# Rotary part of layer 1: ScalarE exchanges the halves, VectorE takes the cosine product, GpSimd the sine product

## The chip, the cores and the metric

One core of a Trainium2 chip runs the whole kernel. The metric is the device time of one execution in microseconds. Before the change it was 678.48 (median of 3 runs, 677.88 to 679.29).

## The reference

The kernel computes four transformer layers on x of 1024 tokens by 256, each layer an attention and a feed-forward part on the same layer norm, added to x. The change is in layer 1's attention: 16 heads of 128 dimensions, rotary embedding on queries and keys, a causal window of 128.

```python
def _apply_rotary(x, cos, sin):
    d2 = x.shape[-1] // 2
    x1, x2 = (x[..., :d2], x[..., d2:])
    return jnp.concatenate([x1 * cos - x2 * sin, x2 * cos + x1 * sin], axis=-1)
...
q = split_heads(hidden_states @ wq)
k = split_heads(hidden_states @ wk)
v = split_heads(hidden_states @ wv)
...
q = _apply_rotary(q, cos, sin)
k = _apply_rotary(k, cos, sin)
valid = (k_pos > q_pos - WINDOW) & (k_pos <= q_pos)
attn = jnp.einsum('bhqd,bhkd->bhqk', q, k) * scale
attn = jnp.where(valid, attn, neg)
attn = jax.nn.softmax(attn, axis=-1)
out = jnp.einsum('bhqk,bhkd->bhqd', attn, v)
return out.transpose(0, 2, 1, 3).reshape(Bsz, Ln, NUM_HEADS * HEAD_DIM) @ wo
```

## The kernel before

The program is written by hand, one queue for each engine; the order in the code is the order of execution, and semaphores tie the queues together. There is no scheduler.

Layer 1 goes head by head (H1 = 16; the first 14, SPLIT, run in loops over pairs, then come the routed and shared experts, then heads 14 and 15). While head h is finished, the queries and keys of head h+1 are prepared. These are four pieces j = 0 to 3, each of 128 dimensions (partitions) by 512 tokens: keys and queries of tokens 0 to 511, then of tokens 512 to 1023. A piece takes this way:

- TensorE projects it (project_qk) into bank j % 2, six products with split weights (L625 to L627). For j = 2 and 3 it first waits until the piece that was in the bank has been read (rope_half).
- ScalarE copies the bank to SBUF (keep_raw, L1349) and counts raw_kept.
- VectorE multiplies the bank by the sine, with the two halves of the partitions exchanged: two instructions of 64 partitions (rotate, L1775 and L1776). The second counts rope_half, which frees the bank.
- GpSimd multiplies ScalarE's copy by the cosine (turn_qk, L2270), waits for rope_half and adds the two (L2275) into kT1 or qT1. That counts qk_ready, for which the scores wait (L821).

Beside this, for head h: row maxima of the scores on VectorE (row_max, L1785), exponents on ScalarE (L1368) in four groups g, transposes of the probabilities on TensorE (turn_probs, L835), their copies on ScalarE (keep_pT, L1335 to L1338), products with the values (L850, L851), the outputs' leading part on ScalarE (keep_oT, L1342) and its rest on VectorE (rest_of_oT, L1792), the output projection on TensorE (project_out, L625 to L627 with 256 columns) and its sum into x on VectorE (L1801).

The weights are split too. ScalarE rounds them (round_wqk L1355, round_wv, round_wo), GpSimd computes the rest (L2232, named rest_of_wqk, rest_of_wv, rest_of_wo) and counts wqk_split, wv_split, wo_split, for which TensorE waits; in heads 11 to 13 VectorE does it for the query and key weights (L1937). Heads come in pairs: behind the second of a pair TensorE also projects the values of the next pair (project_v), and ScalarE copies them (L1330).

VectorE also does the routing of the experts beside the heads: top-k rounds (L1756, L1761) in heads 0 to 8, the last of them and the weights of tokens (L1808 to L1819) in head 9, the row numbers (L1825 to L1839) behind head 10. GpSimd sends rows with indirect DMAs (L2298) in heads 11 to 13 and fetches them (L2303) in heads 14 and 15.

## Time and profile before

| | |
|---|---|
| median of 3 runs | 678.48 us |
| profiled execution, own time | 678.17 us |
| its span, first to last instruction | 676.4 us |
| TensorE busy | 643.2 us, 95% |
| weight loads busy | 504.0 us, 75% |
| VectorE busy | 534.5 us, 79% |
| ScalarE busy | 344.5 us, 51% |
| GpSimd busy | 336.2 us, 50% |
| mean granted TensorE clock | 0.997 |

The busy times are of one profiled execution. PE is TensorE, PEld its weight loads, DVE VectorE, ACT ScalarE, POOL GpSimd; L12 is line 12 of the kernel before. Matmuls are pipelined and their ends are modelled, so that a row of TensorE is best read by its start and the start of the next. Names such as arena, zone and bank are the program's storage: a bank is one of the eight PSUM banks, the others are SBUF.

### The profile page before, as it was taken

To read this page: it belongs to the slowest core of one execution; us is meant where nothing else is said; L and a number is where in the kernel's file an instruction comes from. 1 tells how busy PE (TensorE), PEld (TensorE's weight loads), DVE (VectorE), ACT (ScalarE), POOL (GpSimd) and SP (SyncE) were. 2 spreads that over 40 slices of the span, in tenths; PEclk is the share of its full clock that TensorE was granted. 3 is DMA by queue.
4 is the path that set the end of the run, shared out by engine and by line. 5 is a ranking of instruction groups with operands and counts; after the bars stand their busy time and mean duration, and the time that the engine had idled before them with its cause. 6 is when DMAs were issued, how large, how long until landed. Compare 5 with 4: busy or idle time off the path is not lost.

```text
span 676.4 us, 13522 instructions
## 1 busy us (share of the span) xinstructions
PE 643.2 (95%) x4852; PEld 504.0 (75%) x4852; DVE 534.5 (79%) x1080; ACT 344.5 (51%) x750; POOL 336.2 (50%) x267
## 2 busy tenths in 40 slices
PE   8998999999899999999999999999999999879987
PEld 4446888788478988888898787987868747647766
DVE  4378777698599998988989997667457899679993
ACT  1596212300556485655647564485445583379441
POOL 1063555591457667474866736978429633310000
PEclk9999999999999999999999998999999999999999
DMA  8801000000601001010100101101421300100001
GB/s 258 347 0 64 2 1 1 2 0 0 241 17 41 24 8 39 16 39 23 39 23 8 39 16 50 48 24 30 157 70 48 71 1 0 40 0 1 1 0 63
DMA packets 14792, 31.38 MB, mean 46 GB/s; under 512 B 1853, under 2 KB 8603, under 8 KB 14173
## 3 DMA queue, kind: packets, MB, share of 16 engines
q1 hardware_dynamic: 13069, 27.25, 12.2%
q0 software_dynamic: 1536, 3.15, 1.8%
q8 instruction: 28, 0.46, 0.3%
q10 hardware_dynamic: 144, 0.40, 0.2%
q14 instruction: 15, 0.12, 0.1%
HBM read 26.59 MB, written 5.24 MB: 47 GB/s over the span
## 4 chain that ended last, share of the span: by engine, by line
PE 58%; DVE 16%; issue 11%; ACT 10%; DMA 3%; POOL 2%; SPq 0%; DVEq 0%; POOLq 0%; ACTq 0%
PE bank L625 10%; PE bank L626 8%; PE bank L627 8%; PE bank L615 7%; PE bank L606 5%; PE bank L821 3%; PE bank L851 3%; PE bank L850 2%; PE bank L835 2%; DVE arena L1776 2%; DVE x L1801 2%; DVE arena L1775 2%; PE bank L648 1%; DMA arena<-in_w1s 1%; PE bank L724 1%
## 5 line engine op out<-in xcount | busy, mean ns | idle before, releaser
L625 PE MATMUL bank<-zone 128*128 128x256 f32 (+1 forms) x472 | 167.4, 355 | 12.8 <-DVE arena L1776 3.6
L626 PE MATMUL bank<-zone 128*128 128x256 f32 (+1 forms) x472 | 156.5, 331 | 0.0
L627 PE MATMUL bank<-zone 128*128 128x256 f32 (+1 forms) x472 | 156.3, 331 | 0.0
L625 PEld LDWEIGHTS bank<-zone 128*128 128x128 f32 x472 | 88.8, 188 | 37.8 <-issue 14.6
L2270 POOL TENSOR_TENSOR arena<-arena 128x512 f32<-128x512 f32 x64 | 82.6, 1291 | 63.2 <-ACT arena L1349 63.2
L627 PEld LDWEIGHTS bank<-zone 128*128 128x128 f32 x472 | 89.1, 189 | 9.1
L2275 POOL TENSOR_TENSOR arena<-arena 128x512 f32<-128x512 f32 x64 | 83.8, 1310 | 23.5 <-DVE arena L1776 13.0
L626 PEld LDWEIGHTS bank<-zone 128*128 128x128 f32 x472 | 89.2, 189 | 5.3
L1368 ACT ACTIVATE arena<-arena 128x256 f32<-128x256 f32 (+1 forms) x128 | 62.1, 487 | 30.0 <-DVE arena L1785 29.4
L1785 DVE CUSTOM_DVE_ANT_0 arena<-bank,const 128x256 f32<-128x256 f32 (+1 forms) x128 | 45.7, 404 | 20.0 <-PE bank L821 19.0
L1801 DVE SCALAR_TENSOR_TENSOR x<-bank,arena,x 128x256 f32<-128x256 f32 x128 | 53.0, 473 | 7.4 <-PE bank L627 6.8
L1775 DVE TENSOR_TENSOR arena<-bank,arena 64x512 f32<-64x512 f32 x64 | 44.3, 693 | 16.6 <-ACT arena L1349 15.1
L1349 ACT ACTIVATE arena<-bank 128x512 f32<-128x512 f32 x64 | 37.5, 586 | 28.0 <-PE bank L627 27.9
L851 PE MATMUL bank<-arena 128*128 128x128 f32 x256 | 49.5, 275 | 0.0
L2232 POOL TENSOR_TENSOR zone<-arena,zone 128x512 fp32r<-128x512 f32 (+1 forms) x39 | 40.5, 1047 | 10.8 <-ACT zone L1433 5.1
L850 PE MATMUL bank<-arena 128*128 128x128 f32 x224 | 44.9, 282 | 0.0
L1776 DVE TENSOR_TENSOR arena<-bank,arena 64x512 f32<-64x512 f32 x64 | 43.7, 684 | 0.8
L1330 ACT ACTIVATE arena<-bank 128x512 f32<-128x512 f32 x32 | 19.1, 598 | 48.3 <-PE bank L627 48.3
L851 PEld LDWEIGHTS bank<-arena 128*128 128x128 f32 x256 | 39.9, 191 | 1.9 <-ACT arena L1336 0.6
L821 PE MATMUL bank<-arena 128*32 128x160 f32 x896 | 40.9, 307 | 0.0
L2378 POOL TENSOR_TENSOR arena<-arena,minus_half 128x4 f32<-128x4 f32 x2 | 2.0, 1012 | 75.3 <-DVE arena L2080 75.3
L1088 PE MATMUL bank<-zone 128*128 128x512 f32 x128 | 34.4, 407 | 4.3 <-DVE plain L2062 2.2
(300 smaller groups left out, 1342.1 us busy)
## 6 DMA issues: line engine op xcount, KB each, us to landing
arena<-in_qk SPq DMA_DIRECT2D x16, 256.0 KB
arena<-in_tern SPq DMA_DIRECT2D x1, 3072.0 KB, 21.4
arena<-in_wv SPq DMA_DIRECT2D x8, 256.0 KB, 2.9
arena<-in_wo SPq DMA_DIRECT2D x16, 128.0 KB, 2.1
arena<-in_wr SPq DMA_DIRECT2D x1, 1792.0 KB, 9.9
lB<-in_lB SPq DMA_DIRECT2D x1, 1288.5 KB, 24.0
xg_rows<-arena SPq DMA_DIRECT2D x1, 1024.0 KB
arena<-in_cossin SPq DMA_DIRECT2D x2, 512.0 KB, 5.2
```

What stands on the lines that cost most here:

```text
L625: pe.matmul(dst, lhi, rhi, start=(n == 0), stop=False)
L626: pe.matmul(dst, lhi, rlo, start=False, stop=False)
L627: last = pe.matmul(dst, llo, rhi, start=False, stop=(n == len(terms) - 1 and not open_end))
L821: last = pe.matmul(ps[2 + g % 2][rows_out, at:at + P + 32], qT1[:, t * P + 32 * i:t * P + 32 * i + 32], kT1[:, t * P - P + 32 * i:t * P + ...
L850: pe.matmul(ps[6 + g // 2][:, tok(t % TPB)], v1[:, t - 1, mine], pT1[:, t, 0, :], start=True, stop=False)
L851: last = pe.matmul(ps[6 + g // 2][:, tok(t % TPB)], v1[:, t, mine], pT1[:, t, 1, :], start=(t == 0), stop=True)
L1368: last = act.activation(S1[:, t, lo:], S1[:, t, lo:], ACT.Exp, scale=-1.0, bias=nmax[:, t:t + 1], accum_out=rsum[:, t:t + 1])
L1775: dve.tensor_tensor(qsin[0:64, j, :], ps[j % 2][64:128, :], sinT[64:128, at], ALU.mult)
L1776: dve.tensor_tensor(qsin[64:128, j, :], ps[j % 2][0:64, :], sinT[0:64, at], ALU.mult).then_inc(rope_half, 1)
L1801: last = dve.scalar_tensor_tensor(out=x[:, t, :], in0=ps[bank][:, tt * D:(tt + 1) * D], scalar=rinv[:, t:t + 1], in1=x[:, t, :], op0=ALU.m ...
L2270: pool.tensor_tensor(qraw[:, j, :], qraw[:, j, :], cosT[:, at], ALU.mult).then_inc(cos_done, 1)
L2275: pool.tensor_tensor((kT1, qT1)[j % 2][:, at], qraw[:, j, :], qsin[:, j, :], ALU.add).then_inc(qk_ready, 1)
```

## The change

ScalarE now copies a piece with its halves exchanged, as two copies of 64 partitions. VectorE multiplies the bank by the cosine in one instruction on 128 partitions, and GpSimd multiplies the exchanged copy by a sine table whose signs are exchanged as well. Three orders change with it. On ScalarE the first turned probabilities come ahead of the raw copy of piece 1, and at the end of a head the order is: turned probabilities 2 and 3, first output copy, rounded query and key weights, raw copy of piece 3, second output copy. On VectorE rotation 3 stands behind the first rest of the output. On GpSimd the rest of the query and key weights stands between pieces 2 and 3.

```diff
@@ tables and buffers
-        qsin = m.grid(4, BW)
+        qcos = m.grid(4, BW)
...
-        qraw = m.grid(4, BW)
+        qturn = m.grid(4, BW)
...
-    cossin = np.concatenate([np.tile(np.cos(freq), (2, 1)), np.concatenate([np.sin(freq), -np.sin(freq)], 0)], 1).astype(f32)
+    cossin = np.concatenate([np.tile(np.cos(freq), (2, 1)), np.concatenate([-np.sin(freq), np.sin(freq)], 0)], 1).astype(f32)
@@ ScalarE, keep_raw
-                act.activation(qraw[:, j, :], ps[j % 2], ACT.Copy).then_inc(raw_kept, 1)
+                act.activation(qturn[0:64, j, :], ps[j % 2][64:128, :], ACT.Copy)
+                act.activation(qturn[64:128, j, :], ps[j % 2][0:64, :], ACT.Copy).then_inc(raw_kept, 1)
@@ ScalarE, head
                     if g == 2:
+                        keep_pT(h, 0, base)
                         if more:
                             keep_raw(h + 1, 1)
-                        keep_pT(h, 0, base)
                         keep_pT(h, 1, base)
...
                 if more:
                     keep_raw(h + 1, 2)
                 keep_pT(h, 2, base)
+                keep_pT(h, 3, base)
+                keep_oT(h, 0, base)
+                if more_v:
+                    round_wqk(h + 2)
                 if more:
                     keep_raw(h + 1, 3)
-                keep_oT(h, 0, base)
-                keep_pT(h, 3, base)
                 keep_oT(h, 1, base)
                 if more_v:
-                    round_wqk(h + 2)
                     if c:
                         keep_v(pair + 1)
@@ VectorE, rotate
-                dve.tensor_tensor(qsin[0:64, j, :], ps[j % 2][64:128, :], sinT[64:128, at], ALU.mult)
-                dve.tensor_tensor(qsin[64:128, j, :], ps[j % 2][0:64, :], sinT[0:64, at], ALU.mult).then_inc(rope_half, 1)
+                dve.tensor_tensor(qcos[:, j, :], ps[j % 2], cosT[:, at], ALU.mult).then_inc(rope_half, 1)
@@ VectorE, head
                 if more:
                     rotate(h + 1, 2)
-                    rotate(h + 1, 3)
...
                 for b in range(NB):
                     rest_of_oT(h, b)
+                    if more and b == 0:
+                        rotate(h + 1, 3)
@@ GpSimd, turn_qk
-                    pool.tensor_tensor(qraw[:, j, :], qraw[:, j, :], cosT[:, at], ALU.mult).then_inc(cos_done, 1)
-                    pool.wait_ge(cos_done, h * 4 + (j + 1))
+                    pool.tensor_tensor(qturn[:, j, :], qturn[:, j, :], sinT[:, at], ALU.mult).then_inc(sin_done, 1)
+                    pool.wait_ge(sin_done, h * 4 + (j + 1))
...
-                    pool.tensor_tensor((kT1, qT1)[j % 2][:, at], qraw[:, j, :], qsin[:, j, :], ALU.add).then_inc(qk_ready, 1)
+                    pool.tensor_tensor((kT1, qT1)[j % 2][:, at], qturn[:, j, :], qcos[:, j, :], ALU.add).then_inc(qk_ready, 1)
@@ GpSimd, beside_head
-                turn_qk(h + 1, (2, 3), base)
+                turn_qk(h + 1, (2,), base)
+                if weights:
+                    rest_of_wqk(h + 2)
+                turn_qk(h + 1, (3,), base)
```

ScalarE's queue in the loop, first head of a pair, from the copy of piece 2 to the end of the head. The line numbers are of each kernel's own file. Before:

```order
L1349 ACTIVATE arena<-bank 128x512
L1333 REGISTER_ALU
L1338 ACTIVATE arena<-bank 128x512
L1346 REGISTER_ALU
L1349 ACTIVATE arena<-bank 128x512
L1341 ISA
L1342 ACTIVATE zone<-bank 128x512
L1338 ACTIVATE arena<-bank 128x512
L1342 ACTIVATE zone<-bank 128x512
L1352 ISA
L1354 REGISTER_ALU
L1355 ACTIVATE zone<-arena 128x512
```

The same place in the changed kernel, from the second copy of piece 2:

```order
L1350 ACTIVATE arena<-bank 64x512
L1333 REGISTER_ALU
L1338 ACTIVATE arena<-bank 128x512 x2
L1341 ISA
L1342 ACTIVATE zone<-bank 128x512
L1353 ISA
L1355 REGISTER_ALU
L1356 ACTIVATE zone<-arena 128x512
L1346 REGISTER_ALU
L1349 ACTIVATE arena<-bank 64x512
L1350 ACTIVATE arena<-bank 64x512
L1342 ACTIVATE zone<-bank 128x512
```

The copy of piece 3 has moved behind both turned probabilities, the first output copy and the rounded weights (L1356), and stands right ahead of the second output copy (L1342).

VectorE's queue in the same head, from the last top-k operation to the output's second rest. Before:

```order
L1761 MATCH_REPLACE arena<-arena 7x1024
L1772 REGISTER_ALU
L1774 REGISTER_ALU
L1775 TENSOR_TENSOR arena<-bank,arena 64x512
L1776 TENSOR_TENSOR arena<-bank,arena 64x512
L1772 REGISTER_ALU
L1775 TENSOR_TENSOR arena<-bank,arena 64x512
L1776 TENSOR_TENSOR arena<-bank,arena 64x512
L1869 ISA
L1870 RECIPROCAL arena<-arena 128x8
L1790 REGISTER_ALU
L1792 TENSOR_TENSOR zone<-bank,zone 128x512
```

In the changed kernel:

```order
L1763 MATCH_REPLACE arena<-arena 7x1024
L1774 REGISTER_ALU
L1776 REGISTER_ALU
L1777 TENSOR_TENSOR arena<-bank,arena 128x512
L1869 ISA
L1870 RECIPROCAL arena<-arena 128x8
L1791 REGISTER_ALU
L1793 TENSOR_TENSOR zone<-bank,zone 128x512
L1774 REGISTER_ALU
L1777 TENSOR_TENSOR arena<-bank,arena 128x512
L1791 REGISTER_ALU
L1793 TENSOR_TENSOR zone<-bank,zone 128x512
```

Rotation 3, one product now, has moved from ahead of the reciprocal to between the two rests.

GpSimd's queue in the second head of a pair, from the rest of the output weights to the end of the head. Before:

```order
L2232 TENSOR_TENSOR zone<-arena,zone 128x256
L2269 REGISTER_ALU
L2270 TENSOR_TENSOR arena<-arena 128x512
L2275 TENSOR_TENSOR arena<-arena 128x512
L2269 REGISTER_ALU
L2270 TENSOR_TENSOR arena<-arena 128x512
L2275 TENSOR_TENSOR arena<-arena 128x512
L2278 REGISTER_ALU
L2232 TENSOR_TENSOR zone<-arena,zone 128x512
```

In the changed kernel:

```order
L2234 TENSOR_TENSOR zone<-arena,zone 128x256
L2271 REGISTER_ALU
L2272 TENSOR_TENSOR arena<-arena 128x512
L2277 TENSOR_TENSOR arena<-arena 128x512
L2280 REGISTER_ALU
L2234 TENSOR_TENSOR zone<-arena,zone 128x512
L2271 REGISTER_ALU
L2272 TENSOR_TENSOR arena<-arena 128x512
L2277 TENSOR_TENSOR arena<-arena 128x512
```

The rest of the query and key weights (128x512) now stands ahead of the product and sum of piece 3.

## Rows read from the trace of the kernel before

**Rows 1.** The page: engines' busy time, and costliest groups with idle time before them.

```profile
PE 643.2 (95%) x4852; PEld 504.0 (75%) x4852; DVE 534.5 (79%) x1080; ACT 344.5 (51%) x750; POOL 336.2 (50%) x267
...
L2275 POOL TENSOR_TENSOR arena<-arena 128x512 f32<-128x512 f32 x64 | 83.8, 1310 | 23.5 <-DVE arena L1776 13.0
...
L1349 ACT ACTIVATE arena<-bank 128x512 f32<-128x512 f32 x64 | 37.5, 586 | 28.0 <-PE bank L627 27.9
...
L1776 DVE TENSOR_TENSOR arena<-bank,arena 64x512 f32<-64x512 f32 x64 | 43.7, 684 | 0.8
```

**Rows 2.** Busy time of heads 3 and 4 by engine: PE, PEld, DVE, ACT, POOL.

```profile
268.60:308.30 39.70, 39.39 (x355) 34.04 (x358) 35.61 (x83) 24.51 (x65) 25.58 (x22) 1.00 0.10 26
```

**Rows 3.** Timeline of TensorE, head 4: start, us, line, idle time before.

```profile
268.59 1.02 PE L821 MATMUL bank<-arena 128*32 128x160 f32 x24
269.55 0.38 PE L625 MATMUL bank<-zone 128*128 128x256 f32 x1
...
282.17 0.50 PE L625 MATMUL bank<-zone 128*128 128x512 f32 x1 [0.16 <-DVE arena L1776]
...
287.47 0.39 PE L850 MATMUL bank<-arena 128*128 128x128 f32 x2
...
289.69 1.02 PE L821 MATMUL bank<-arena 128*32 128x160 f32 x24
290.79 0.38 PE L625 MATMUL bank<-zone 128*128 128x256 f32 x1
...
293.49 0.28 PE L626 MATMUL bank<-zone 128*128 128x256 f32 x1
293.61 0.28 PE L627 MATMUL bank<-zone 128*128 128x256 f32 x1
293.96 0.49 PE L625 MATMUL bank<-zone 128*128 128x512 f32 x1
```

**Rows 4.** Timeline of ScalarE, head 4; the last row is from the experts.

```profile
280.02 0.58 ACT L1349 ACTIVATE arena<-bank 128x512 f32<-128x512 f32 x1
...
283.05 0.51 ACT L1368 ACTIVATE arena<-arena 128x256 f32<-128x256 f32 x1
...
284.87 0.57 ACT L1349 ACTIVATE arena<-bank 128x512 f32<-128x512 f32 x1
285.35 0.58 ACT L1338 ACTIVATE arena<-bank 128x512 f32<-128x512 f32 x1
...
290.06 0.62 ACT L1355 ACTIVATE zone<-arena 128x512 fp32r<-128x512 f32 x1
...
490.98 0.59 ACT L1421 ACTIVATE arena<-bank 80x512 f32<-80x512 f32 x1 [0.57 <-PE bank L951]
```

**Rows 5.** Timeline of VectorE, head 4.

```profile
281.43 0.68 DVE L1776 TENSOR_TENSOR arena<-bank,arena 64x512 f32<-64x512 f32 x1
...
290.09 1.24 DVE L1792 TENSOR_TENSOR zone<-bank,zone 128x512 fp32r<-128x512 f32 x2
```

**Rows 6.** Timeline of GpSimd, head 4.

```profile
292.52 2.55 POOL L2232 TENSOR_TENSOR zone<-arena,zone 128x512 fp32r<-128x512 f32 x2
```

**Rows 7.** Timeline of VectorE, heads 10 and 11.

```profile
401.97 0.68 DVE L1776 TENSOR_TENSOR arena<-bank,arena 64x512 f32<-64x512 f32 x1
...
415.72 0.20 DVE L1825 COPY arena<-bank 128x56 f32<-128x56 f32 x1
```

**Rows 8.** Timeline of GpSimd, heads 12 and 13.

```profile
444.05 1.28 POOL L2270 TENSOR_TENSOR arena<-arena 128x512 f32<-128x512 f32 x1 [2.91 <-ACT arena L1349]
...
472.27 0.76 POOL L2232 TENSOR_TENSOR zone<-arena,zone 128x256 fp32r<-128x256 f32 x1
```

**Rows 9.** Timeline of VectorE, before head 0.

```profile
189.38 0.94 DVE L1910 TENSOR_TENSOR arena<-arena 128x48 f32<-128x48 f32 x1
...
194.48 0.16 DVE L1910 TENSOR_TENSOR arena<-arena 128x8 f32<-128x8 f32 x1
```

**Rows 10.** Busy time by stretch, as rows 2; the third number from the end is the clock.

```profile
417.00:418.00 1.00, 1.00 (x4) 0.57 (x2) 0.90 (x6) 0.00 (x0) 0.00 (x0) 0.50 0.55 211
```

More of the change, by code:

```diff
@@ L235, in build @@
         affT_ready = sem("affT_ready")
-        xT1_kept, cos_done = sem("xT1_kept"), sem("cos_done")
+        xT1_kept, sin_done = sem("xT1_kept"), sem("sin_done")
         xT_hi, wqk_hi, wqk_split, wo_hi, wo_split, raw_kept, oT1_hi = (
@@ L2304, in fetch_rows, with beside_head @@
                                             bounds_check=SLOTS, oob_is_err=False).then_inc(gathered[n % NT // TPB], 16)
-            def beside_head(h, base=HEAD0, between=lambda: None):
+            def beside_head(h, base=HEAD0, between=lambda: None, weights=True):
                 turn_qk(h + 1, (0, 1), base)
@@ L2314, in _ @@
                     beside_head(i * 2 + c)
-                    rest_of_wqk(i * 2 + (c + 2))
                     if c == 0:
@@ L2324, in _ @@
                 send_rows(early)
-                beside_head(h, between=lambda: send_rows(later))
-                if h == SPLIT - 4:
-                    rest_of_wqk(h + 2)
+                beside_head(h, between=lambda: send_rows(later), weights=h == SPLIT - 4)
                 if h % 2 == 0:
```

## The prediction

> **What bounds the kernel now.** I read the page first. TensorE is busy 95% of the span, VectorE 79%, ScalarE 51%, GpSimd 50% [rows 1]. The change touches only layer 1's attention, heads 0 to 15, from 181 to 537 us, so I went on by stretches. In a pair of heads in the middle TensorE is busy 39.39 of 39.70 us at the full granted clock [rows 2]. So these 39.7 us hardly depend on the other engines, and all that this change can win is in the few places where TensorE waits for one. TensorE's timeline of head 4 (the first of a pair, "even" below) shows three [rows 3]. The third projection, at 282.17, has 0.16 us of idle time before it. The output projection begins at 290.79, 1.10 after the scores' row at 289.69, against 0.96 from 268.59 to 269.55 in a head that does not wait: 0.14. From the last product at 293.61 to the next head's projection at 293.96 are 0.35, where the pitch of these products is 0.12 (293.49 to 293.61): 0.23. Matmul ends are modelled, and a first product behind a wait takes some 0.1 longer, so together I count 0.7 us in a pair. The second, "odd", head has no such wait.
>
> What ends them: the first, VectorE's second sine product (281.43, over at 282.11), behind ScalarE's copy of 280.02 [rows 4, 5]. The second, the output's rest on VectorE at 290.09, which stood behind both products of rotations 2 and 3 [rows 5]. The third, GpSimd's rest of the query/key weights, the first of the two at 292.52 and so over at 293.8 [rows 6].
>
> Two stretches differ. In heads 9 and 10 VectorE is late from its top-k work; TensorE's third projection of head 10 waits for the sine product that ends at 402.65 [rows 7]. From head 12 into the routed experts GpSimd's row sends bind: it starts at 444.05 behind ScalarE's first copy, works almost without a pause from there on, and TensorE's outputs wait for the rest of the output weights that it computes at 472.27 [rows 8].
>
> **The change, part by part.** Each of 64 rotations trades two VectorE products on 64 partitions (684 ns) for one on 128. VectorE's cost goes by columns: its two 128x512 ops on a bank and SBUF at 290.09 take 1.24 together [rows 1, 5]. I take 0.69 for the new one, so VectorE gets back 0.69 each, 44 us in all, nearly all of it beside a full TensorE. ScalarE writes two 64x512 copies for one 128x512 of 586 ns. A copy of 64 partitions isn't in the trace; one of 80 took 0.59, as one of 128, and consecutive ones start 0.48 apart (284.87, 285.35) [rows 1, 4]. So the second copy costs +0.48, with bounds of 0.24 (half, if partitions counted) and 0.60 (no overlap). GpSimd has its two products of 1.3 us as before; the first starts 0.48 later, but the sum behind it no longer waits for VectorE, which cost 13.0 us in 15 places [rows 1]. I let that come out even.
>
> *Even heads 0 to 6 (numbers of head 4).* ScalarE's copies for rotation 0 end at 281.08, 0.48 later than before. The cosine product ends at about 281.9 instead of 282.11, and TensorE could go on at 282.0: the first wait is gone. Then come two exponents (0.5 each, the kind of 283.05), the first turned probabilities (0.4), the two copies for rotation 1, over at 283.4, and their product, over at 284.2. TensorE wants that bank after the third projection and some small products, by 284.4. The third pair of copies ends 1.25 later than before (three times 0.48, less the 0.19 that ScalarE waited before 283.05). So group 2's turned probabilities, over at 285.93 before, are over at 287.2. TensorE needs them at 287.47, or 287.25 without the first wait [rows 3, 4]. There is 0.05 left, and I allow 0.1 of stall. Next ScalarE does group 3's probabilities, the first output copy (over at 288.6), the weights (289.1, where it was 290.68), the copies for rotation 3 (290.2) and the second output copy (290.7). VectorE's first rest is over by 289.3, so the second wait goes; its second is over at 291.6 (was 291.33), in time for the third output, which is 1.4 behind 290.65. GpSimd: two rotations from 281.1 (5.2), output weights 0.7, rotation 2 (2.6), the query/key weights over at 291 and not 293.8: the third wait goes. Rotation 3 ends at 293.6, before the scores that stand behind the next projection. I take 0.6 of the 0.7; four even heads (0, 2, 4, 6): -2.4, bounds 0 and -3.2.
>
> *Odd heads.* There ScalarE waits for TensorE before its copies (most of its 28.0 us of idle time before them [rows 1]) and VectorE's row maxima set the exponents, so the second copies fall into idle time: 0, bounds -0.2 and +0.5 for all.
>
> *Heads 8 to 10.* In head 8 VectorE has rotation 3 between the two rests and waits for its copies, so what follows begins 0.3 later, as in head 4. Then rotation 0 of head 9 is 0.69 shorter: -0.37 at head 9's third projection. Rotation 0 of head 10 gives 0.69 more. But in head 10, without top-k work, the second rest came as soon as its copy was there; now it stands behind the copies and the product of rotation 3, 0.7 later by my count of ScalarE's chain as above. Behind it are the row maxima, eight adds and the copy at 415.72 for which TensorE waits [rows 7]. So the 0.69 of head 10 is spent again, and with it, since VectorE's chain is unbroken there, most of the 0.37: 0 in all, bounds -1.4 and +0.8.
>
> *Heads 12 and 13.* The copies put GpSimd's start at 444.05 back by 0.47; some 0.2 of it returns where its first sum waited for VectorE. So +0.27 at 472.27, and what follows (scattered rows, then the expert weights, ScalarE's first Silu) hangs on it [rows 8]. TensorE's own gains are swallowed by the same wait. Bounds 0 and +0.5.
>
> *Heads 14 and 15.* The first product and the four adds behind it are over 0.2 earlier. But ScalarE's copies for rotation 3 now lie ahead of the second output copy, VectorE gets to the row maxima and adds 0.2 later, and head 15, with no projections to fill it, waits for those: +0.2, bounds -0.2 and +0.7.
>
> *Start (rotations of head 0).* VectorE's rotations there are over 0.35 earlier. Behind them is a row of small comparisons, and one of these took 0.94 at 189.38; one of the last, at 194.48 with GpSimd idle, took 0.16 [rows 9]. The slow ones ended as a GpSimd product ended. GpSimd's own chain ends up to 0.27 later, so I take 0, bounds -0.35 and +0.27. The Trainium skill, "SBUF — State Buffer", section "Who interferes with whom", states that a VectorE instruction with two SBUF inputs contends with a GpSimd instruction that reads SBUF. The trace agrees (0.94 for 0.16 us). By that rule the start gives 0, without it -0.35.
>
> The sum: -2.4 + 0 + 0 + 0.27 + 0.2 + 0 = -1.9 us. The profiled execution took 678.17 (span 676.4), so 676.3. The median of the three runs, 678.48, is 0.31 above it; with half of that I predict 676.5.
>
> **Rivals.**
> *ScalarE becomes the bound of the even heads (slower).* If a 64-partition copy doesn't overlap its follower, its pitch is 0.60, and group 2's probabilities come 1.97 late (six times 0.60, less three times 0.48 and 0.19) where 1.32 are free: a stall of 0.65 in each even head, which eats the 0.6 gained. The late second rest then costs 0.7 in each of heads 8 and 10, 0.5 in head 12 and 0.7 in head 14: +2.6, so 680.8. It decides from a pitch of about 0.50. For it: only 0.05 us of room. Against: 512 columns show 0.48.
> *The waits are passed on.* TensorE comes 0.2 earlier and meets the next release, which ScalarE's chain fixes (284.2 for 284.4, 287.2 for 287.25). If half of each even gain goes so: -1.2 + 0.5 = -0.7, so 677.5 to 677.8.
> *All of VectorE's time counts.* Even heads give 0.8 each (-3.2), heads 9 and 10 their 1.4, the start 0.35, and nothing is lost later: -4.9, 673.3. For it: VectorE's 79%, and the 13.0 us that GpSimd waited for it. Against: TensorE's 39.39 of 39.70.
>
> **Chances.** Forecast 0.50 (its own range 674.9 to 677.8), passed on 0.20, all counts 0.12, ScalarE bound 0.18. A measurement here tells 0.2% (1.36 us) from no change. Faster: 0.8 of the forecast's 0.50, and the 0.12, is 0.52. Slower: nearly all of the ScalarE case, 0.17. Same: 0.31. Range 673.8 to 679.8; it leaves out the far ends of the first and third rivals.
>
> One thing lies outside: TensorE's granted clock was 0.50 around 417 us [rows 10], behind a pause in which it waited for VectorE at the end of head 10. Half speed for some 3 us costs about 1.6. That pause becomes longer, so I expect it again; a second such stretch, or none, would shift the result by as much.
>
> **What would show it.** Right: VectorE's product x64 at 0.69 and its busy time down 44 us; ScalarE's up by 64 copies more at a pitch of 0.48; a middle pair of 39.0 to 39.1 us instead of 39.65; in head 4 no wait before the third projection, the output or the next head's first projection, and at most 0.1 for group 2's probabilities; from head 12's start to 485 us 0.3 more. Wrong: pairs still at 39.6, TensorE waiting 0.5 for L1338 (probabilities) in each even head, or TensorE's third output waiting for the rest of L1792.

## The result and the profile after

The changed kernel took 685.09 us (median of 4, 683.85 to 686.04), the kernel before 678.61 (677.88 to 679.29): ratio 1.0099, interval 1.0079 to 1.0120. It is slower, by 6.5 us; I had predicted 676.5, 2 us faster, and 685.09 lies outside the range.

Single executions far off the others (1272.34 and 799.71 of the kernel before, 3574.05 of c_w) were slow ones and are left out of all ratios below.

The page of the kernel after, engine totals and costliest groups (line, engine, shapes, count, busy and mean ns, idle time before and its main releaser), beside [rows 1]:

```profile
PE 644.5 (94%) x4852; PEld 503.7 (74%) x4852; DVE 487.5 (71%) x1016; ACT 387.3 (57%) x814; POOL 337.1 (49%) x267
...
L2277 POOL TENSOR_TENSOR arena<-arena 128x512 f32<-128x512 f32 x64 | 84.1, 1313 | 7.7 <-DVE arena L1777 1.9
L1777 DVE TENSOR_TENSOR arena<-bank,arena 128x512 f32<-128x512 f32 x64 | 44.0, 688 | 56.2 <-ACT arena L1350 52.5
...
L850 PE MATMUL bank<-arena 128*128 128x128 f32 x224 | 44.5, 281 | 3.6 <-ACT arena L1338 3.5
...
L1349 ACT ACTIVATE arena<-bank 64x512 f32<-64x512 f32 x64 | 38.0, 594 | 15.2 <-PE bank L627 13.8
```

The parts that I had priced by duration came out: VectorE's one product takes 688 ns and its busy time falls by 47 us, GpSimd's wait for VectorE is nearly gone (13.0 to 1.9). Two rows are new. VectorE's product waits 52.5 us in all for ScalarE's second copy (L1350), and TensorE waits 3.5 us for ScalarE's turned probabilities (L1338).

Busy time in the middle pair, by the same two matmuls as [rows 2] to within 0.1 us (39.80 us before). [rows 2] calls the pair heads 3 and 4, but the stretch begins with the scores for head 4, which stand near the end of head 3, and ends with those for head 6 near the end of head 5: it holds head 4, which is even, and head 5, which is odd.

```profile
268.54:308.88 40.34, 39.60 (x355) 34.10 (x358) 29.82 (x76) 29.96 (x74) 25.84 (x22) 1.00 0.09 26
```

I had said 39.0 to 39.1 instead of 39.65, and 39.6 as the sign that I was wrong. Those were between two matmuls 0.16 closer together, so that they stand here for 39.2, 39.80 and 39.8. It is 40.34. TensorE's timeline of head 4, beside [rows 3]; both heads start within 0.05 us of each other, so the times compare directly:

```profile
282.15 0.50 PE L625 MATMUL bank<-zone 128*128 128x512 f32 x1 [0.19 <-DVE arena L1777]
...
284.93 0.50 PE L625 MATMUL bank<-zone 128*128 128x512 f32 x1
...
287.32 0.60 PE L835 MATMUL bank<-const,arena 128*128 128x128 f32 x4
288.46 0.48 PE L850 MATMUL bank<-arena 128*128 128x128 f32 x2 [0.54 <-ACT arena L1338]
...
290.66 1.02 PE L821 MATMUL bank<-arena 128*32 128x160 f32 x24
291.61 0.38 PE L625 MATMUL bank<-zone 128*128 128x256 f32 x1
...
294.56 0.28 PE L627 MATMUL bank<-zone 128*128 128x256 f32 x1
294.67 0.39 PE L625 MATMUL bank<-zone 128*128 128x512 f32 x1
```

The first wait is still there. The products for group 2 start at 288.46 and not at 287.47. The other two waits are gone as predicted: 0.95 from the scores' row at 290.66 to the output, and 0.11 to the next head. ScalarE in the same head, beside [rows 4]:

```profile
280.09 0.59 ACT L1349 ACTIVATE arena<-bank 64x512 f32<-64x512 f32 x1
280.70 0.59 ACT L1350 ACTIVATE arena<-bank 64x512 f32<-64x512 f32 x1
281.31 0.51 ACT L1369 ACTIVATE arena<-arena 128x256 f32<-128x256 f32 x1
...
282.47 0.37 ACT L1336 ACTIVATE arena<-bank 128x256 f32<-128x256 f32 x1
282.86 0.60 ACT L1349 ACTIVATE arena<-bank 64x512 f32<-64x512 f32 x1
283.47 0.59 ACT L1350 ACTIVATE arena<-bank 64x512 f32<-64x512 f32 x1
284.09 0.60 ACT L1338 ACTIVATE arena<-bank 128x512 f32<-128x512 f32 x1
...
287.73 1.08 ACT L1338 ACTIVATE arena<-bank 128x512 f32<-128x512 f32 x2
```

Starts are 0.61 apart, not 0.48, after either copy. The instruction ahead of the pair loses its overlap as well: from L1336 to L1349 are 0.39, where a copy of 128 partitions follows L1336 after 0.264. So a rotation costs ScalarE 0.61 + 0.61 + 0.12 instead of 0.48, 0.86 more with a predecessor close ahead, and group 2's probabilities start at 287.73, 2.38 later than in [rows 4], where I had 1.25. VectorE's products follow the copies:

```profile
281.41 0.69 DVE L1777 TENSOR_TENSOR arena<-bank,arena 128x512 f32<-128x512 f32 x1 [1.48 <-ACT arena L1350]
...
284.18 0.69 DVE L1777 TENSOR_TENSOR arena<-bank,arena 128x512 f32<-128x512 f32 x1 [1.22 <-POOL arena L2277]
...
291.07 0.69 DVE L1777 TENSOR_TENSOR arena<-bank,arena 128x512 f32<-128x512 f32 x1 [1.04 <-ACT arena L1350]
291.69 0.69 DVE L1793 TENSOR_TENSOR zone<-bank,zone 128x512 fp32r<-128x512 f32 x1
```

The first is over at 282.10, where the second sine product of [rows 5] was over at 282.11: what VectorE saves ScalarE has spent. The second is over only at 284.87, and TensorE's fourth projection goes from 284.68 to 284.93. Its row names a GpSimd sum (L2277) as releaser, but that is inferred: the count of qk_ready for which this product waits was reached in the head before, and what it lacked was raw_kept, by the copy of 283.47 that ends at 284.06. (The last two rows are for a comparison further down.)

Whole stretches, from starts in TensorE's timelines (the order of its 4852 matmuls is the same in both kernels). "Again" are two later profiles of the same kernels, each from another session:

| stretch, us | before | after minus before | again: after minus before |
|---|---|---|---|
| start of layer 1 to head 0 | 22.95 | +0.35 | +0.73 |
| heads 0 to 7 | 158.66 | +1.34 | +1.36 |
| heads 8 to 10 | 60.13 | +2.00 | +1.97 |
| head 11 | 23.95 | -1.12 | +0.79 |
| head 12 to the experts | 40.18 | +0.55 | -1.76 |
| experts to layer 2 | 57.01 | +1.50 | +0.21 |
| layer 2 to 590 us | 52.86 | +1.62 | -1.62 |

Read it by rows 2 and 3: they repeat to 0.03 us. The other rows do not, and stretches at half clock are one reason. In the kernel before one begins at 417 [rows 10], in the one after at 588.7, in the kernel after again at 422.5. The kernel before again has two, at 467.7 (row 5) and 590.6. In the kernel after:

```profile
590.00:592.00 2.00, 2.00 (x6) 0.50 0.00 0
```

What such a stretch costs can be read from the profiles of all runs. The last row of the table is 1.59 to 1.65 longer than in the first profile in the eleven that have one there, and at most 0.05 longer in the others. Head 11 is 0.87 shorter without one in the kernel before, and 1.04 shorter in the kernel after. So in the first comparison it moved from a place where it cost 0.9 to 1.0 to one where it costs 1.6, which is some 0.6 of the 6.5 us.

The kernel before took 678 us in two of the sessions and 684 to 685 in the three others, mostly by more time from head 13 on. So all that follows compares ratios within a session, or pairs of heads. It is not the chip alone: by the record one and the same chip gave 677.69 in one session and 684.95 in another. Part of it is the clock. In executions of the kernel before the granted clock averaged 0.998 in the session of 677.69 and 0.994 to 0.995 in the longer ones; profiles with one, two and three stretches at half clock show 0.997, 0.995 and 0.992. That is one to one and a half stretches more in an execution, by my estimate 1.6 to 2.4 of the 7 us.

### The profile page after: what moved, and what is told of

Read it like the earlier page. It is cut to its first block, busy times and chain, and to the rows that moved or that the text cites. A ratio compares the mean times of both kernels' runs of the same rounds, so it can differ in the third digit from the quotient of the medians.

```text
span 682.1 us, 13522 instructions
## 1 busy us (share of the span) xinstructions
PE 644.5 (94%) x4852; PEld 503.7 (74%) x4852; DVE 487.5 (71%) x1016; ACT 387.3 (57%) x814; POOL 337.1 (49%) x267
## 4 chain that ended last, share of the span: by engine, by line
PE 54%; ACT 18%; issue 11%; DVE 10%; POOL 3%; DMA 3%; ACTq 0%; SPq 0%; POOLq 0%; DVEq 0%
PE bank L625 9%; PE bank L626 7%; PE bank L627 7%; PE bank L615 7%; PE bank L606 5%; ACT arena L1369 3%; PE bank L821 3%; PE bank L850 2%; PE bank L851 2%; ACT arena L1349 2%; ACT arena L1350 2%; DVE x L1802 2%; PE bank L835 1%; PE bank L648 1%; DMA arena<-in_w1s 1%
## 5 line engine op out<-in xcount | busy, mean ns | idle before, releaser
L2277 POOL TENSOR_TENSOR arena<-arena 128x512 f32<-128x512 f32 x64 | 84.1, 1313 | 7.7 <-DVE arena L1777 1.9
L1777 DVE TENSOR_TENSOR arena<-bank,arena 128x512 f32<-128x512 f32 x64 | 44.0, 688 | 56.2 <-ACT arena L1350 52.5
L1349 ACT ACTIVATE arena<-bank 64x512 f32<-64x512 f32 x64 | 38.0, 594 | 15.2 <-PE bank L627 13.8
L1330 ACT ACTIVATE arena<-bank 128x512 f32<-128x512 f32 x32 | 19.1, 597 | 45.3 <-PE bank L627 45.2
L851 PEld LDWEIGHTS bank<-arena 128*128 128x128 f32 x256 | 40.0, 192 | 1.9 <-ACT arena L1336 0.6
L850 PEld LDWEIGHTS bank<-arena 128*128 128x128 f32 x224 | 35.0, 191 | 6.8 <-issue 3.9
```

The costliest lines, as they stand in the source:

```text
L850: pe.matmul(ps[6 + g // 2][:, tok(t % TPB)], v1[:, t - 1, mine], pT1[:, t, 0, :], start=True, stop=False)
L851: last = pe.matmul(ps[6 + g // 2][:, tok(t % TPB)], v1[:, t, mine], pT1[:, t, 1, :], start=(t == 0), stop=True)
L1349: act.activation(qturn[0:64, j, :], ps[j % 2][64:128, :], ACT.Copy)
L2277: pool.tensor_tensor((kT1, qT1)[j % 2][:, at], qturn[:, j, :], qcos[:, j, :], ALU.add).then_inc(qk_ready, 1)
```

## The experiments

For each the length of the middle pair is given, between the same two matmuls: 39.80 before, 39.81 when profiled again, 40.34 after and 40.36 again. Runs of one session share the runs of the kernel before.

**Which part costs (kernel before 684.24).**

x1_halves, the kernel before with

```
-                act.activation(qraw[:, j, :], ps[j % 2], ACT.Copy).then_inc(raw_kept, 1)
+                act.activation(qraw[0:64, j, :], ps[j % 2][0:64, :], ACT.Copy)
+                act.activation(qraw[64:128, j, :], ps[j % 2][64:128, :], ACT.Copy).then_inc(raw_kept, 1)
```

> The kernel before, with ScalarE's raw copy cut into two copies of 64 partitions, without the exchange (input and output on the same partitions). Everything else as before. Theory A (two 64-partition copies cost ScalarE about 0.7 to 0.85 us more than one of 128, by partition count, whatever the exchange): pitch 0.61, TensorE waits in each even head for rope_half and turned probabilities, time 684 to 692 us. Rival A2 (only the exchange, reading one half of the partitions and writing the other, loses the overlap): pitch 0.48, time 680 to 684. Rival B (the new orders cost the time, not the copies): at most 680.

Measured: 697.82, ratio 1.0226 (1.0166 to 1.0286), pair 41.70. The times that I expected in these four were for a kernel before of 678; even scaled to that, 693.8, this one lies above all of them. The pitch is that of theory A. ScalarE's timeline:

```profile
283.29 0.57 ACT L1349 ACTIVATE arena<-bank 64x512 f32<-64x512 f32 x1
283.87 0.59 ACT L1350 ACTIVATE arena<-bank 64x512 f32<-64x512 f32 x1
284.49 0.51 ACT L1369 ACTIVATE arena<-arena 128x256 f32<-128x256 f32 x1
```

0.58 and 0.62 apart, without any exchange. But here the instruction ahead keeps nearly all of its overlap: from a full copy (L1338) to L1349 are 0.49 (median of 15), where full copies are 0.48 apart; with the exchange and the same order (x2_exchange, next) it is 0.62.

x2_exchange, the changed kernel with the old orders on ScalarE, VectorE and GpSimd (the reverse of the order hunks of the diff).

> The changed kernel with the three queues in the old orders: only the rotary work is redistributed (two exchanged copies, one cosine product, sine on GpSimd). Theory A (the copies cost the time): still slower than before by 4 us or more, 683 to 690. Rival B (the new orders cost the time): 675 to 679.

Measured: 702.99, ratio 1.0281 (1.0240 to 1.0322), pair 42.40. The sign is theory A's, the size above it. With the old orders the change costs 2.6 us a pair net of what VectorE gains; the new ones take 2.1 of it back.

x3_orders, the kernel before with the new orders alone (copies and products as before).

> The kernel before with the new orders alone (probabilities ahead of raw copy 1, output copy and weights ahead of raw copy 3, rotation 3 between the rests, weights between pieces 2 and 3 on GpSimd); rotary work as before. Theory A: the waits for the rest of the output and for the query/key weights go, about 0.35 to 0.45 us in each pair: 676 to 678, not slower than before. Rival B: 682 or more.

Measured: 687.33, ratio 1.0038 (1.0017 to 1.0058), pair 39.90. The gain expected did not come: even heads take 0.25 longer, odd ones 0.17 less. With two sine products, rotation 3 between the two rests is a new wait. VectorE, then TensorE:

```profile
289.89 0.69 DVE L1776 TENSOR_TENSOR arena<-bank,arena 64x512 f32<-64x512 f32 x1 [0.31 <-ACT arena L1349]
290.59 0.68 DVE L1777 TENSOR_TENSOR arena<-bank,arena 64x512 f32<-64x512 f32 x1
291.31 0.69 DVE L1793 TENSOR_TENSOR zone<-bank,zone 128x512 fp32r<-128x512 f32 x1
```

```profile
292.06 0.38 PE L625 MATMUL bank<-zone 128*128 128x256 f32 x1 [0.40 <-DVE zone L1793]
```

x4_one_copy, the changed kernel with one full copy, the exchange left out:

```
-                act.activation(qturn[0:64, j, :], ps[j % 2][64:128, :], ACT.Copy)
-                act.activation(qturn[64:128, j, :], ps[j % 2][0:64, :], ACT.Copy).then_inc(raw_kept, 1)
+                act.activation(qturn[:, j, :], ps[j % 2], ACT.Copy).then_inc(raw_kept, 1)
```

> The changed kernel with one ScalarE copy of 128 partitions in place of the two; the exchange of halves is left out, so queries and keys are rotated wrongly. VectorE's relief and the new orders stay. Theory A: all that the change can win without its price on ScalarE, 0.6 to 0.8 us in each pair and more in heads 8 to 10: 672 to 676. Rival B: 682 or more. Rival C (VectorE's relief is worth nothing because TensorE is full): 676 to 678, as with the new orders alone.

Measured: 677.26, ratio 0.9890 (0.9846 to 0.9935). Busy time of the pair:

```profile
266.12:305.08 38.96, 38.96 (x356) 34.05 (x359) 29.54 (x75) 24.16 (x65) 25.76 (x22) 1.00 0.10 27
```

TensorE never pauses: 38.96 of 38.96. The relief of VectorE and the new orders together are worth 0.84 us a pair, what I had found as waits (0.7) and a little more. The copies' price is then 40.34 - 38.96 = 1.38 a pair. The four runs together: all of the loss sits in ScalarE's copies.

**Was the size of the pitch the whole error (next session, kernel before 677.69)?**

y_double pays exactly the price that I had predicted, +0.48: two full copies. The first goes where VectorE's product comes afterwards.

```
+                act.activation(qcos[:, j, :], ps[j % 2], ACT.Copy)
+                act.activation(qturn[:, j, :], ps[j % 2], ACT.Copy).then_inc(raw_kept, 1)
```

> The changed kernel, but each rotation's values are copied twice by ScalarE on all 128 partitions in place of the two exchanging copies on 64 (the first copy goes where VectorE's product comes afterwards). The exchange is left out. A second full copy costs ScalarE 0.48 us, exactly what the prediction had put on the second half copy. Theory A (the copies' price on ScalarE, 0.73 to 0.86 a rotation and not 0.48, is the whole error): the rest of the prediction's sum then holds, and this kernel lies near 0.997 of the kernel before. In the profile L1349 and L1350 start 0.48 apart, and a middle pair of heads takes about 39.1 us. Rival B (price in proportion, no slack on ScalarE: 0.989 with no second copy, 1.010 with 0.78 us more): 1.002, a middle pair at 39.7. Rival C (the number of instructions counts, whatever their partitions): as the changed kernel, 1.010.

Measured: 677.52, ratio 0.9990 (0.9973 to 1.0007), pair 39.32. ScalarE's timeline and the pair:

```profile
284.91 0.61 ACT L1349 ACTIVATE arena<-bank 128x512 f32<-128x512 f32 x1
285.39 0.62 ACT L1350 ACTIVATE arena<-bank 128x512 f32<-128x512 f32 x1
285.87 0.63 ACT L1338 ACTIVATE arena<-bank 128x512 f32<-128x512 f32 x1
```

```profile
267.87:307.19 39.32, 39.32 (x356) 34.07 (x359) 29.84 (x75) 27.95 (x73) 25.75 (x22) 1.00 0.09 27
```

At that price a pair gains 0.48, nearly the 0.6 of my sum; at 0.86 it loses 0.54. But only 0.31 of the 0.48 lies in the even head, where my sum had 0.6: the waits before the third projection and the next head are gone, the one before the output (0.12) is not. The other 0.2 lies in the odd head, where my sum had nothing. Adding 0.48 to ScalarE's rotations cost 0.36 a pair (38.96 to 39.32), adding some 0.4 more cost 1.02. The price is not in proportion: there is slack, and then none. The whole kernel gained less than the 0.3% expected; my 0.9971 lies just outside its interval, no change within.

x6_relief_old, one full copy and the old orders.

> VectorE's one product in place of two and a single copy on 128 partitions (the exchange is left out), with the orders of the kernel before on all three queues. Same work as the kernel that came out at 0.989, only the order differs. Theory A (the new orders only repair what the late copies break, and do next to nothing otherwise): 0.989 to 0.993. Rival (the new orders carry the gain once VectorE is relieved): 0.996 or more, with the waits before the output projection and for the query/key weights back in every even head, 0.7 us a pair.

Measured: 672.81, ratio 0.9914 (0.9880 to 0.9948), pair 39.17. So the new orders are worth 0.2 a pair once VectorE is relieved, 2.1 when ScalarE is late, and nothing (-0.1) with the two sine products of before. They repair what the copies break: the exchange costs 3.2 a pair with the old orders (39.17 to 42.40) and 1.4 with the new.

**Where can an exchange be had for nothing?**

h_odd: copies, product and orders of the changed kernel in odd heads and at the start, those of the kernel before in even heads (a flag for each head; GpSimd subtracts where the sine comes from VectorE; VectorE's loop over heads 11 to 13 is written out).

```
+                if turned:
+                    act.activation(qturn[0:64, j, :], ps[j % 2][64:128, :], ACT.Copy)
+                    act.activation(qturn[64:128, j, :], ps[j % 2][0:64, :], ACT.Copy).then_inc(raw_kept, 1)
+                else:
+                    act.activation(qturn[:, j, :], ps[j % 2], ACT.Copy).then_inc(raw_kept, 1)
```

> Whole computation. The exchange by ScalarE, one product on VectorE and the new orders in odd heads only (rotations for heads 2, 4, ... and at the start); in even heads the copies, two sine products and orders of the kernel before. Theory A (in even heads ScalarE is the bound and the exchange costs 0.76 each, in odd ones it lies in idle time; the changed kernel gained 0.24 in each odd head from 1 to 7 and 1.1 in head 11): 0.9965, about 2.3 us less than before. Rival (an exchange costs in any head, and the gain of the odd heads was only what the even ones had lost a little earlier): 1.002 or more.

Measured: 678.50, ratio 1.0010 (0.9993 to 1.0028), pair 39.71. The exchange is free in odd heads, but its gain there is 0.1 and not 0.24. The other 0.1 goes with the early weights: c_w further down, which changes nothing else, gains 0.1 in each odd head, and h_odd_w, next, 0.2. The miss is mine; the rival was half right.

h_odd_w: the same, and in even heads the weights early, on GpSimd between pieces 2 and 3, on ScalarE moved here from behind the second output copy:

```
                 keep_pT(h, 3, base)
+                if more_v:
+                    round_wqk(h + 2)
                 keep_oT(h, 1, base)
```

> As the kernel with the exchange in odd heads only, and in the even heads ScalarE rounds the query/key weights before the second output copy, and GpSimd computes their rest between rotations 2 and 3. Theory A (the wait of 0.23 us before the next head's first projection goes, nothing else moves): 0.2 us less for each of seven even heads, 0.9945. Rival (the second output copy comes 0.5 later, and with it VectorE's second rest and TensorE's third output): 0.997 to 1.0.

Measured: 677.82, ratio 0.9996 (0.9981 to 1.0011), pair 39.38. Each even head gains 0.22, as expected, and each odd one 0.2 (theory A: nothing), 1.8 us from head 0 to head 9. The whole does not show it: in its profile the start took 1.2 longer and the experts to layer 2 took 1.3 longer than in the first profile of the kernel before.

**Why is the pitch 0.61 (third session of experiments, kernel before 685.13)?** Both kinds of half copy change two things at once, the number of partitions and the one at which they start.

p_half, the changed kernel with a copy of partitions 0 to 63 and then a full one, the exchange left out:

```
+                act.activation(qcos[0:64, j, :], ps[j % 2][0:64, :], ACT.Copy)
+                act.activation(qturn[:, j, :], ps[j % 2], ACT.Copy).then_inc(raw_kept, 1)
```

> The changed kernel with other copies: ScalarE first copies partitions 0 to 63 (64x512, to where VectorE's product comes afterwards), then all 128 partitions (128x512). The exchange is left out. No copy begins at another partition than the one before it. Theory 1 (ScalarE gives up the overlap with its predecessor where the start partition changes, in the bank or in the destination): both starts come 0.48 after the one before (L1349 to L1350, L1350 to the next), and the time is that of two full copies, 0.999 of the kernel before. Theory 2 (a copy of fewer than 128 partitions gives up its overlap with what follows): L1349 to L1350 0.60, L1350 to the next 0.48, and about 1.002 to 1.004.

Measured: 678.61, ratio 0.9904 (0.9879 to 0.9930), pair 39.24. ScalarE's timeline:

```profile
286.56 0.63 ACT L1356 ACTIVATE zone<-arena 128x512 fp32r<-128x512 f32 x1
287.08 0.58 ACT L1349 ACTIVATE arena<-bank 64x512 f32<-64x512 f32 x1
287.56 0.58 ACT L1350 ACTIVATE arena<-bank 128x512 f32<-128x512 f32 x1
288.03 0.59 ACT L1342 ACTIVATE zone<-bank 128x512 fp32r<-128x512 f32 x1
```

0.52, 0.48, 0.47: a copy of 64 partitions overlaps with both neighbours if it starts at partition 0 like them (64 times, median 0.477). So it is not the count. The overlap of some 0.12 is lost wherever the partition at which an instruction starts to read or to write differs from that of the one before: twice in x1_halves (into 64 to 127 and out of it), three times with the exchange (it reads from 64 at once), so 0.48 + 3 x 0.12, or 0.84 more. Either alone is enough: into the exchange only the read moves (0.39 for 0.264 from L1336, 15 times), and out of it only the write (0.61 from L1350 to L1338, 30 times). Starts other than 0 and 64 were not tried. VectorE shows the same in the rows of x3_orders above: the sine products, which change their partitions, start 0.70 and 0.72 apart, where a full product and the rest behind it start 0.62 apart (291.07 and 291.69, in VectorE's rows of the kernel after).

The Trainium skill, "VectorE: DVE Perf Modes", section "Two Vector instructions with no wait between them", states as a model that a VectorE instruction whose input or output starts in another group of 32 partitions than the last access to that memory waits until all earlier ones are finished. The traces agree for VectorE, and by these runs the rule holds for ScalarE as well, of which the page says nothing. Carried over to ScalarE, at a loss of 0.12 for each of the three changes, it would have given +0.84 and the right sign. That loss could be read in the kernel before: VectorE's two sine products start 0.71 apart there (64 times), and its two full instructions of [rows 5], 1.24 together, 0.56.

The whole kernel was faster than I expected, 0.9904 for 0.999, in a session in which the kernel before itself was 1% longer. What part of that is the session's is open.

c_w, the kernel before with the weights early alone (ScalarE as in the diff of h_odd_w, GpSimd's rest of them between rotations 2 and 3).

> Whole computation. The kernel before with one thing of the change: ScalarE rounds the query/key weights before the second output copy, and GpSimd computes their rest between rotations 2 and 3. Theory A (the wait of 0.23 us before the first projection of the head after an even one goes, and the price, a second output copy 0.5 later, falls into TensorE's third output's slack): 0.2 us less for each of seven pairs, 0.998. Rival (the odd heads gain as well, 0.2 each, as they did with the new orders alone): 0.996. Rival (the late output copy is waited for): 1.001.

Measured: 683.55, ratio 0.9985 (0.9970 to 1.0001), pair 39.48. The third wait is gone; the next head's projection follows the last product after 0.11:

```profile
292.06 0.28 PE L627 MATMUL bank<-zone 128*128 128x256 f32 x1
292.17 0.40 PE L625 MATMUL bank<-zone 128*128 128x512 f32 x1
```

A pair gains 0.32, 0.22 in even heads and 0.1 in odd ones. As a whole, 0.9985 for the 0.998 expected, it is at the edge of what can be told.

h_best, as h_odd_w, but at the start and in head 15 everything as before.

> Whole computation. As the kernel with the exchange in odd heads and the weights early in even ones, but at the start and in head 15 as before: head 0's rotations with one copy and two sine products, and in head 15 ScalarE's first output copy ahead of the last turned probabilities. Theory A (in head 15 the changed order put the first output copy 0.9 us later and TensorE's third output 0.6 later; the exchange at the start costs 0.1 to 0.3): 0.9980, of which 2.1 us less up to the end of head 13 and 0 from there on. Rival (the late output copy in head 15 was waited out elsewhere): as the other, 0.9996.

Measured: 679.45, ratio 0.9919 (0.9895 to 0.9942), pair 39.39. It is faster than the kernel before, by 5.7 us where 1.4 were expected. The heads up to head 9 give 1.8 of that; from head 12 to the experts it takes 2.5 less than the next run, the kernel before in the same session.

b_again, the kernel before, unchanged.

> The kernel before, for its profile on this chip. If the start of layer 1 (up to head 0's first scores) is 0.9 us longer here too, that part of the other kernels' time belongs to the chip and not to them. If it is as in the first profile, it is theirs.

Measured: 685.26, pair 39.81. Its start is 0.74 longer too, so that part of the other kernels' time isn't theirs. From head 12 to the experts it takes 3.7 longer than in the first profile, of which head 13 alone has 2.7. VectorE stands still ahead of a row maximum, beside GpSimd's row sends:

```profile
465.16 0.42 DVE L1785 CUSTOM_DVE_ANT_0 arena<-bank,const 128x256 f32<-128x256 f32 x1 [3.15 <-remote]
```

TensorE is busy 0.89 us of the 3 from 464 to 467, and from 467.7 its granted clock is 0.50:

```profile
468.00:470.00 2.00, 2.00 (x6) 0.50 0.00 0
```

At the price found above, that second stretch at half clock is some 1.6 of the 3.7 us.

**What was left (last session, kernel before 684.95).**

a_tail, the changed kernel with head 15's first output copy ahead of the last turned probabilities again (`if more:` around the moved line).

> Whole computation. The changed kernel with one order put back: in head 15 ScalarE's first output copy stands ahead of the last turned probabilities again. Theory A (that swap put the copy 0.9 us later and TensorE's third output of head 15 0.6 later): 0.6 to 0.9 us less than the changed kernel, all of it between head 15's output and layer 2, TensorE's wait for the output's second rest 0.8 instead of 1.4. Rival (VectorE is late there from the fetched rows, and the order does not matter): no difference, the wait stays 1.4.

Measured: 687.60, ratio 1.0031 (1.0015 to 1.0047). VectorE's wait for that copy in a_again, then here:

```profile
540.90 0.69 DVE L1793 TENSOR_TENSOR zone<-bank,zone 128x512 fp32r<-128x512 f32 x1 [1.04 <-ACT zone L1342]
```

```profile
539.38 0.69 DVE L1796 TENSOR_TENSOR zone<-bank,zone 128x512 fp32r<-128x512 f32 x1 [0.48 <-ACT zone L1342]
```

The wait is shorter, but the gain of 0.6 to 0.9 that I expected did not come: the time is that of a_again. In this profile VectorE stands 1 us before the second rest, and TensorE has a stretch at half clock from 539.4 on, one of three. The swap delays the copy; that it costs time isn't shown.

a_again, the changed kernel unchanged.

> The changed kernel itself. If its loss lies in the even heads and heads 8 to 10 (4.2 us of the 5.7 by the milestones), the ratio is 1.006 to 1.012 on any chip, and each even head from 2 to 8 takes 0.76 us longer than in the kernel before, each odd one 0.24 less. If the loss depended on the chip, the pairs would differ by more than 0.05 us from that.

Measured: 687.21, ratio 1.0033 (1.0018 to 1.0047), pair 40.36. Up to head 10 it loses 3.3 us to the kernel before, as in the first profiles (+0.76 in each even head from 2, -0.24 in each odd one). The pairs repeat as expected, but the ratio is below the 1.006 that I expected as the least: b_again, in another session of 685 us, lost 3.7 us between head 12 and the experts against the first profile, and the changed kernel lost 2.0 there.

h_best2, the same kernel as h_best.

> The mixed kernel again (exchange in odd heads from 1 to 13 only, weights early everywhere), on this chip. Theory A (it gains 0.42 us a pair, 1.9 us up to head 9, and the rest of its 0.8% came from row sends that bound the kernel before on that chip): 0.996 to 0.998 where the kernel before takes about 678, 0.991 to 0.994 where it takes 684 or more. Rival (the gain in pairs is lost again at the end, as the kernel with the exchange at the start showed): 0.9995.

Measured: 680.40, ratio 0.9935 (0.9914 to 0.9956), pair 39.40. The 0.4 us a pair repeat. They are 2 of the 4.5 us; the rest lies from head 13 on, where the kernel before loses more in a session of 685 us, and this profile has no stretch at half clock before the last microseconds, where b_again has two. That it gains in a session of 678 us was not measured; h_odd_w, which differs at the start and in head 15, did not.

## Why the prediction was wrong, step by step

*The step that failed: "the second copy costs +0.48".* It was a term of the sum that was mis-sized, and every later step of the even heads hung on it. It measured 0.86 where something stands close ahead. My upper bound, 0.60, assumed the new copy's own overlap lost; but the copy behind it and the instruction ahead of it lose theirs as well. The row that I had taken it from (80 partitions, 0.59, [rows 4]) starts at partition 0 like its neighbours. I had read it as a price of partial copies; for a change of partition it was no bound at all. y_double shows that with 0.48 the sign of the sum holds, 0.48 gained of the predicted 0.6 in a pair, and with it two of the three waits. That the total comes so near is in part luck, for 0.2 of it is the odd head's.

*Even heads, -2.4.* Heads 0 to 7 came out at +1.34. First wait: gone by my sum, in fact unchanged (282.15 for 282.17). Fourth projection: on time by my sum, 0.25 late. Group 2's probabilities: 0.05 of room; their products in fact start 1.0 later (288.46 for 287.47), of which 0.7 is their own stall (1.14 behind 287.32, 0.43 before). Output projection and query/key weights: both waits gone, as predicted, 0.37 won against 1.1 lost, so head 4 takes 0.76 longer.

*Odd heads, 0.* Right that the copies fall into idle time: h_odd costs nothing there. Wrong that nothing could be won: each odd head is 0.2 shorter in x4_one_copy, y_double and the changed kernel alike.

*Heads 8 to 10, 0.* +2.00. Heads 8 and 10 are even heads, with the same late probabilities; I had looked only at VectorE's chain there. In head 10:

```profile
410.46 0.49 PE L850 MATMUL bank<-arena 128*128 128x128 f32 x2 [0.57 <-ACT arena L1338]
```

*Heads 12 and 13, +0.27; 14 and 15, +0.2; start, 0.* +0.55, +1.50 and +0.35 in the first profiles, -1.76 (from 12), +0.21 and +0.73 in the second: these stretches vary by more than the terms, so they are neither confirmed nor refuted. In head 15 I had missed that the diff swaps the output copy there too. At the start the kernel before differs from itself by 0.74, more than my bounds of -0.35 and +0.27. The slow comparison of [rows 9] has 48 columns and the fast one 8; with 48 one took 0.20 at 194.56, so the reading stands.

*The rival "ScalarE becomes the bound of the even heads".* It happened, at a chance of 0.18, and my range ended at 679.8, below this rival's own 680.8. It named the place, the releaser and the sign; its price of 2.6 was too small for the same reason (1.97 late where 2.38 were measured), and the loss up to head 10 alone is 3.3 us. The deciding point held: 0.48 is a gain, 0.61 a loss. The rival "all of VectorE's time counts" is near what x4_one_copy shows, with the exchange left out: a pair 0.84 shorter, 5.2 us up to head 10. VectorE was worth relieving, and ScalarE was the wrong engine to pay.

*The rest of the 6.5 us.* 3.3 up to head 10 repeat. About 3 more in the first comparison came from the start and from behind head 10, and did not repeat. The moved stretch at half clock is some 0.6 of them; the rest stays open.

## What to carry to other kernels

Before work goes from the busiest engine to an idle one, look at the head (or stage) in which the idle one is least idle: ScalarE was busy 51% of the span, but in each even head the copies could put group 2's probabilities back by 1.3 us at no cost, and they put them back by 2.4. Price a new instruction by its pitch among its neighbours, both ahead and behind, and where no row has its shape or its start partition, let the range reach to no overlap on every side. A reordering should be tried with the old work first: here it mostly repaired what the new work broke, and only one part of it (the weights earlier) gained with the old work, 0.32 us a pair.

## What the runs showed of the hardware

ScalarE's instructions of 512 columns from a bank start 0.48 us apart (64 times in y_double, and as often with 64 partitions from partition 0 in p_half), and 0.58 to 0.62 where the start partition, of the read or of the write, changes from one to the next; both take 0.59 each. The loss of 0.12 appears also behind a short one (0.264 to 0.39 from L1336). VectorE's products took 0.69 on 64 and on 128 partitions, at 0.70 to 0.72 and at 0.62 apart.

A stretch at a granted clock of 0.50 (1.2 GHz) cost 1.6 us between layer 2 and 590 us, and 0.9 to 1.0 us in head 11. The one of b_again at 467.7 came behind a pause in which TensorE was busy 0.89 of 3 us.

VectorE stood still for up to 4.3 us (x4_one_copy) and ScalarE for up to 5.0 (x1_halves) beside GpSimd's row sends and fetches, with a releaser "remote" or "issue". All eleven profiles of the three longer sessions have such pauses of over 0.9 us, the kernel before among them, and none of the six of the two shorter ones has any. I have no cause for it.
